# Cross-attention kernel on one core: other lists of the last tiles, with the last slots' maxima next to scores or products

## What is computed

```python
Q = (query @ w_q.T) ; K = (key @ w_k.T) ; V = (value @ w_v.T)      # 16 heads of 32
scores = einsum('bhqd,bhkd->bhqk', Q, K) / sqrt(32)
attn = softmax(scores, axis=-1)
ctx = einsum('bhqk,bhkd->bhqd', attn, V)
out = ctx @ w_o.T + b_o
x = out + query
return (x - mean(x)) * rsqrt(var(x) + 1e-5) * ln_gamma + ln_beta
```

## Time and profile before

| what | value |
|---|---|
| time, median of 3 runs | 539.16 us (538.46 to 540.26) |
| the profiled execution's own time | 539.97 us |
| its span | 537.9 us |
| TensorE busy | 526.6 us (98%) |
| VectorE, ScalarE, GpSimd busy | 474.8, 423.8, 444.2 us |
| mean granted clock of TensorE | 0.998 of full speed |

### The profile page before, as it was taken

One profiled execution on the slowest core, in us unless ns is written; L12 is line 12 of the kernel. 1 busy time (PEld: TensorE's weight loads), 2 busy tenths in 40 slices (PEclk: granted clock), 3 DMA queues, 4 the chain that ended last, 5 costly groups with the idle time before them and its releaser, 6 DMA issues.

```text
span 537.9 us, 12626 instructions
## 1 busy us (share of the span) xinstructions
PE 526.6 (98%) x4522; PEld 372.8 (69%) x4522; DVE 474.8 (88%) x877; ACT 423.8 (79%) x795; POOL 444.2 (83%) x387
## 2 busy tenths in 40 slices
PE   8989999999999999999999999999999999999994
PEld 7765677777667666766676677667767777777563
DVE  7876768999999989999999988899989989998887
ACT  7647768888888888888888888888888888877783
POOL 1725866899889989898989899999999998877956
PEclk9999999999999999999999999999999999999999
DMA  8952332343234332443243324333433332222123
GB/s 301 271 167 72 91 98 68 118 124 124 74 122 132 124 102 90 132 127 97 91 132 104 117 98 127 105 115 105 124 96 108 123 125 73 61 76 85 45 83 117
DMA packets 56750, 61.12 MB, mean 114 GB/s; under 512 B 29168, under 2 KB 29168, under 8 KB 56688
## 3 DMA queue, kind: packets, MB, share of 16 engines
q1 hardware_dynamic: 56688, 60.32, 36.0%
HBM read 39.58 MB, written 16.78 MB: 105 GB/s over the span
## 4 chain that ended last, share of the span: by engine, by line
PE 92%; DVE 3%; DMA 1%; issue 1%; ACT 1%; SPq 0%; DVEq 0%
PE ps_q L430 32%; PE ps_o L436 28%; PE ps_s L389 12%; PE ps_s L362 8%; PE ps_q L289 5%; PE ps_s L373 3%; PE ps_o L289 3%; PE ps_s L289 2%; DMA max_rows<-max_turned 1%; PE ps_s L296 1%; DVE stats L797 1%; DVE z L793 1%; DVE q_lo L707 0%; DVE y L819 0%; SPq L224 0%
## 5 line engine op out<-in xcount | busy, mean ns | idle before, releaser
L430 PE MATMUL ps_q<-x_hi,wq_lo 64*128 64x512 f32 x448 | 180.9, 404 | 0.2 <-issue 0.2
L436 PE MATMUL ps_o<-wo_hi,c_lo 64*128 64x512 f32 x448 | 180.9, 404 | 0.0
L430 PE MATMUL ps_q<-x_hi,wq_hi 64*128 64x512 f32 x448 | 175.3, 391 | 0.0
L436 PE MATMUL ps_o<-wo_hi,c_hi 64*128 64x512 f32 x448 | 175.2, 391 | 0.0
L430 PE MATMUL ps_q<-x_lo,wq_hi 64*128 64x512 f32 x448 | 175.1, 391 | 0.0
L436 PE MATMUL ps_o<-wo_lo,c_hi 64*128 64x512 f32 x448 | 174.6, 390 | 0.0
L930 POOL TENSOR_TENSOR c_lo<-c_raw,c_hi 128x512 fp32r<-128x512 f32 x63 | 81.7, 1296 | 50.5 <-ACT c_hi L519 50.5
L430 PEld LDWEIGHTS ps_q<-x_hi,wq_lo 64*128 64x128 f32 x448 | 82.6, 184 | 54.8 <-DVE z L793 46.1
L937 POOL TENSOR_TENSOR x_raw<-x_raw,bias_row 128x512 f32<-128x512 f32 x64 | 103.6, 1621 | 0.0
L430 PEld LDWEIGHTS ps_q<-x_hi,wq_hi 64*128 64x128 f32 x448 | 82.6, 184 | 9.9
L436 PEld LDWEIGHTS ps_o<-wo_lo,c_hi 64*128 64x128 f32 x448 | 82.8, 185 | 7.9
(11 more groups left out here) (109 smaller groups left out, 1089.4 us busy)
## 6 DMA issues: line engine op xcount, KB each, us to landing
xT_raw<-in_xT SPq DMA_DIRECT2D x64, 256.0 KB, 3.2
x_raw<-in_x SPq DMA_DIRECT2D x64, 256.0 KB, 2.8
out<-y SPq DMA_DIRECT2D x64, 256.0 KB, 2.3
max_rows<-max_turned SPq DMA_DIRECT2D x128, 16.0 KB
ctx_raw<-in_ctxT SPq DMA_DIRECT2D x4, 256.0 KB, 4.1
wk_raw<-in_wkT SPq DMA_DIRECT2D x4, 256.0 KB, 4.3
wq_raw<-in_wqT SPq DMA_DIRECT2D x4, 256.0 KB, 5.8
wv_raw<-in_wvT SPq DMA_DIRECT2D x4, 256.0 KB, 6.7
```

Source lines behind the costliest of these rows:

```text
L430: return nc.tensor.matmul(ps_q[:, 0, :], w[l][half, k, dims], x_[r][half, qc % 2, k, :], start=(half is lower and k == 0 and step == 0), s ...
L436: return nc.tensor.matmul(ps_o[:, 0, :], cx[l][half, k, tile], wo[r][half, k, :], start=(half is upper and k == 0 and step == 0), stop=(ha ...
```

## The change

Only the lists of the tail change, no instruction is added or removed.

- TensorE: `subtract_max(61)` moves behind the output tile 56, to stand ahead of `score(63)`. `subtract_max(62)` and `(63)` move out of the middle of the tiles 58 and 59, to stand right behind `combine_values(61)` and `(62)`. The steps k of the tiles 60 and 61 alternate as 0 and 1, then 2, then 3, in place of 0 to 2, then 3.
- ScalarE: `exponentiate(62)` goes ahead of `log_sums(61)`, and `exponentiate(63)` ahead of `log_sums(62)`; `negate_max(62)` goes ahead of `exponentiate(61)`, `negate_max(63)` ahead of all work of slot 61; `normalise(54)`, `normalise(56)` and the deviations move.
- VectorE: `divide(60)` goes behind the maxima of slot 62, `turn_max(62)` ahead of the residual of tile 56, `divide(61)` behind the statistics of 56 and 57.
- GpSimd: `scale(54)` goes ahead of `context_to_lo(60)`, `scale(56)` behind `context_to_lo(62)`.

```diff
@@ tensor
+            project_output(56, range(KT))
             subtract_max(61)
-            project_output(56, range(KT))
             score(63)
             project_output(57, range(KT))
             combine_values(61)
-            project_output(58, first_half)
             subtract_max(62)
-            project_output(58, second_half)
+            project_output(58, range(KT))
             combine_values(62)
-            project_output(59, first_half)
             subtract_max(63)
-            project_output(59, second_half)
+            project_output(59, range(KT))
             combine_values(63)
-            project_output(60, range(KT - 1))
-            project_output(61, range(KT - 1))
-            project_output(60, (KT - 1,))
-            project_output(61, (KT - 1,))
+            for ks in (first_half, (2,), (3,)):
+                project_output(60, ks)
+                project_output(61, ks)
             project_output(62, range(KT))
             project_output(63, range(KT))
@@ scalar
             invert_deviation(54)
+            invert_deviation(55)
+            negate_max(62)
             exponentiate(61)
+            normalise(54)
             context_to_hi(60)
-            negate_max(62)
-            normalise(54)
-            invert_deviation(55)
             normalise(55)
+            negate_max(63)
+            exponentiate(62)
             log_sums(61)
-            negate_max(63)
             invert_sums(61)
-            exponentiate(62)
             invert_deviation(56)
             context_to_hi(61)
-            normalise(56)
+            exponentiate(63)
             log_sums(62)
             invert_sums(62)
-            exponentiate(63)
+            invert_deviation(57)
+            normalise(56)
             context_to_hi(62)
-            invert_deviation(57)
             log_sums(63)
@@ vector
             turn_scores(62)
-            divide(60)
             half_maxima(62)
             fold_halves(62)
+            divide(60)
+            turn_max(62)
             add_residual(56)
-            turn_max(62)
             turn_scores(63)
             half_maxima(63)
             fold_halves(63)
             add_residual(57)
             turn_max(63)
-            divide(61)
             statistics(56)
             statistics(57)
+            divide(61)
@@ gpsimd
             add_bias(62)
             shift_mean(54)
+            shift_mean(55)
             add_bias(63)
+            scale(54)
             context_to_lo(60)
-            shift_mean(55)
-            scale(54)
             scale(55)
             shift_mean(56)
             context_to_lo(61)
+            context_to_lo(62)
             scale(56)
-            context_to_lo(62)
             for i in (59, 60, 62):
                 scale(i)
```

## The result

The changed kernel takes 541.87 us (median of 11 runs, 541.11 to 543.42) against 539.16 us in the same session. The ratio is 1.0049, 95% interval 1.0038 to 1.0060: slower by half a per cent, 2.0 to 3.2 us (2.7 by the medians). The profiled execution took 542.84 us with a span of 541.1 us.

A forecast was written before the change was run, and what follows sets the result against it. TensorE bounds the kernel up to tile 60's last step, then 11.05 us of VectorE and a store follow. TensorE's sum of 0 to +0.2, ScalarE's delays and GpSimd's holds put tile 60's residual +2.3 late: 541.5 us, range 539.5 to 542.9.

The forecast's parts named there:

- The wait ahead of the maximum of 61: TensorE, head of the tail: subtract_max(61)'s wait for its transfer gets covered by tile 56's matmuls, -0.54.
- change of shape: TensorE at score(63): the subtraction beside it costs 0.34, the score a plain 0.25 step; alone it cost 0.43; together -0.2.
- score(63) held by divide(60): TensorE could score at 504.0 but waits until 505.3, since VectorE's divide(60) now follows the maxima of slot 62: +1.3.
- TensorE's own sum: TensorE up to the products of slot 63: gains and the wait at score(63) nearly cancel, 0 to +0.2.
- High part of 62: ScalarE: the high part of slot 62 starts at about 518.95 in place of 517.82, 1.1 late.
- divide(63), +0.3: VectorE: divide(63) can start at 521.4, 0.3 late, after ScalarE is free only at 519.5 for slot 63.
- VectorE held by GpSimd: End of tail: GpSimd's operations hold scale_centred(58), low part of 63 and finish(58); step 3 of tile 60 +1.6, residual +2.3.
- The last stretch: From the residual of tile 60 to the end of finish(63), mostly VectorE: stays 11.05 us long.
- By which 0.55 or 0.85: How long after GpSimd's operation a held VectorE operation ends: 0.55 by the profile row, used for +2.3; 0.85 by the skill, +3.1.
- the dearer case: Rival at the tail's end: every new hold of VectorE by GpSimd 0.3 dearer, +3.2, 542.4 us; chance 0.09.
- ready at 519: GpSimd: scale(56), ready at 519, stands behind the low part of 62, so its two operations fall into VectorE's last stretch.
- have to wait for TensorE's products anyway: Other edits: earlier turn_max(62) and negate_max gain 0, since the subtractions of 62 and 63 wait for TensorE's products.

The follow-up runs named there:

- The second experiment: Changed kernel with GpSimd's scale(56) alone put back ahead of context_to_lo(62); ratio to the kernel before 1.0059 (1.0039 to 1.0078), tail +2.60.
- the one kernel that was run twice: Kernel before with subtract_max(61) alone moved behind output tile 56, next to score(63); ratios 0.9992 and 0.9978, tail -0.76 and -0.78.

## Why the prediction was right

**541.5 us were forecast, in a range of 539.5 to 542.9; 541.87 were measured.** The difference to before was forecast at 2.3 and is 2.49 in the tail. The mechanism was the one forecast, and its terms came out as follows, all counted in the tail.

- *The wait ahead of the maximum of 61, -0.54*: gone. With the change of shape, -0.74 was expected at `score(63)` if nothing holds it; the kernel with that move alone shows 3.89 against 4.58, -0.69.
- *score(63) held by divide(60), +1.3*: 1.22 of idle; the score starts 1.37 later than in the kernel with the maximum of 61 alone moved (5.26 against 3.89). The next tile starts 0.67 late against 0.6.
- *TensorE's own sum, 0 to +0.2* at the products of slot 63: +0.14. From the products of 61 to those of 62 it gains 0.19, as forecast, and from there to those of 63 0.37 in place of 0.2. In the kernel before, the last matmul ahead of the products of 63 (517.48) takes a step of 0.50, where it is 0.32 ahead of those of 62: they waited about 0.18 for the exponential that ends at 517.92. The prediction doesn't count this wait, which ScalarE's new list takes away; without it the sum would have been +0.32, so that it fell in the range is in part luck.
- *High part of 62, +1.1*: +1.37 (519.86 less 500.78, against 517.82 less 500.11). **This term was too small.** The exponential was taken with the step of 0.91 up to the next instruction, where a conversion follows. Where a logarithm follows, the step was 1.06 and 1.05 (rows below). Only the second of the two stands on this path, 0.14. What is ahead of it on ScalarE doesn't hold it: the conversion of 61, at 515.16, would let it go 0.52 later, at 515.68, but the subtraction of 63 (515.38, 0.49 long) ends only at 515.87. That subtraction comes 0.11 later in the tail than worked out, and the exponential 0.04 later behind it. With rounding this makes the 0.24 beyond the forecast 1.13.

```profile
511.48 1.03 ACT L605 ACTIVATE probs<-ps_s 128x1024 f32<-128x1024 f32 x1 [0.91 <-PE ps_s L373]
512.54 0.60 ACT L558 ACTIVATE inverse<-ps_s 64x512 f32<-64x512 f32 x1
...
515.92 1.03 ACT L605 ACTIVATE probs<-ps_s 128x1024 f32<-128x1024 f32 x1
516.97 0.60 ACT L558 ACTIVATE inverse<-ps_s 64x512 f32<-64x512 f32 x1
...
519.86 0.62 ACT L516 ACTIVATE c_hi<-c_raw 128x512 fp32r<-128x512 f32 x1
520.50 0.60 ACT L558 ACTIVATE inverse<-ps_s 64x512 f32<-64x512 f32 x1
```

- *divide(63), +0.3*: +0.67, by the same 0.24 and by 0.1 more: the conversion at 519.86 takes 0.64 up to the logarithms of 63, where 0.52 was read ahead of the logarithm of a single column.
- *VectorE held by GpSimd*: `scale_centred(58)` 1.10, low part of 63 1.75, `finish(58)` 1.77, in the order that was worked out. Step 3 of tile 60 +1.87 (+1.6), its residual +2.52 (+2.3). That the low part of 63 is held as `scale_centred` is, which was an assumption, held.
- *The last stretch, 11.05*: 11.02.
- *By which 0.55 or 0.85*: the Trainium skill (SBUF — State Buffer, section "Who interferes with whom") says that whoever issues first keeps the shared ports for its whole instruction, and the four pairs above agree. The 115 ns after the release, from which the dearer case was estimated, are given in the Trainium skill (SBUF — State Buffer, section "A bandwidth-pool intuition that's wrong") for descriptors that GpSimd writes while VectorE holds the ports, not for an operation of VectorE held by one of GpSimd. For that pair they are not seen: VectorE's held operations end 0.55 behind GpSimd's, 0.14 to 0.2 less than the 0.69 to 0.75 that they take alone. So no row stands behind the 0.3 of the dearer case, and its sum is given once as +3.1 and once as +3.2.

One thing the prediction had wrong without its number suffering: it laid the holds to GpSimd's order, as if `scale(56)` were "ready at 519" by chance. The second experiment shows that its old place would have been no better with ScalarE's new list; beside ScalarE's new list it is the pair that costs, while beside ScalarE's old list GpSimd's order costs 0.89 by itself. And the moves of the maxima of 62 and 63 pay both only in kernels where TensorE is late by its stall: there the steps between the products are 4.43 and 4.43 in place of 4.62 and 4.80. Without the stall one of the moved subtractions waits 0.40 to 0.49 for its transfer (four kernels). That the subtractions of 62 and 63 "have to wait for TensorE's products anyway" was thus true of this kernel and not of the better ones.

## What to carry to other kernels

Where each engine runs a list of its own, a list is right or wrong only beside the others: GpSimd's old order lost nothing beside ScalarE's old list and 2.5 us of waiting beside its new one, and ScalarE's list alone cost 7 us. Before moving an instruction of GpSimd into a gap, look at what VectorE does in that gap; in these profiles an operation of each with two operands from SBUF was a turn, not an overlap, and here, near the end of the program, nothing was left to hide it. Measure a change of a few tenths of a microsecond from a fixed instant inside the profile: the tail of the one kernel that was run twice repeated to 0.02 us, where its medians lay 0.6 apart.

## What the runs showed of the hardware

- TensorE idle for 1.22, 1.56 and 1.58 us stayed at a granted clock of 1.00; idle for 4.55 us it fell to 0.50 within the idle time (0.84 over 520 to 524, with TensorE idle from about 520.7) and came back near 529.3, 4 us after work had begun again. The fall cost 2.0 us.
- An exponential of 128x1024 on ScalarE takes 0.91 up to a following conversion and 1.05 up to the logarithms of the sums. A conversion of 128x512 takes 0.52 up to a normalisation and 0.64 up to the same logarithms, so some 0.12 to 0.15 more shows ahead of these logarithms, whichever comes first. Why isn't settled; no run was made for it.
- Every operation of VectorE with two operands from SBUF that one of GpSimd held, in the tails of all these profiles, ended 0.53 to 0.56 behind it, and took 0.83 to 1.78 in place of 0.69 to 0.75.
- Products, then the subtraction of the maximum, then a full tile cost 0.57 and 0.42 in the tail of the changed kernel (510.38, 510.95, 511.37) and 0.57 and 0.43 in the first slots, so a price of the shape changes could be read at one end of the program and used at the other.
